# A layer norm moved to the head of VectorE's step, ahead of an earlier group's norm

## The reference

```
x = layernorm(x + sage(x, src, dst))        # three layers
x = layernorm(x + gat(x, edges))            # two attention layers
x = layernorm(x + jk(x, src, dst))          # four layers, maximum over them, one linear layer
x = layernorm(x + gcn(x, edges))            # three layers
```

## Time and profile before

| | |
|---|---|
| median of the runs | 7616.2 us |
| the profiled execution | 7673.8 us, span 7672.0 us |
| VectorE (DVE) | 4630.7 us busy, 60% of the span |
| TensorE (PE) | 4978.3 us busy, 65% |
| ScalarE (ACT) | 3048.8 us busy, 40% |
| GpSimd (POOL) | 3996.4 us busy, 52% |
| mean granted clock of TensorE | 0.798 |

### The profile page before, as it was taken

The page is one execution under the profiler, slowest core; times in us unless marked ns, Lnnn a source line. Parts: engine busy times, 40 slices in busy tenths (PEclk is TensorE's granted clock), DMA queues, the critical chain, the costliest instruction groups (busy, mean ns, idle before and its releaser), DMA issues. The chain is left out here.

```text
span 7672.0 us, 87356 instructions
## 1 busy us (share of the span) xinstructions
PE 4978.3 (65%) x23920; PEld 3346.6 (44%) x23924; DVE 4630.7 (60%) x13648; ACT 3048.8 (40%) x6979; POOL 3996.4 (52%) x3991
## 2 busy tenths in 40 slices
PE   6898887869989824676423444433799995579211
PEld 4666665535568602576322222221455553356111
DVE  4777666223356526667675456656899995545444
ACT  3555554533323202443343333333677773245000
POOL 4565554544344374655655655656233334654766
PEclk9999998989989755697555766766899998789555
DMA  6997665767756422686443466654577774566322
GB/s 146 236 243 231 204 207 175 238 194 243 234 179 202 124 53 53 173 249 190 127 119 105 128 112 119 120 105 87 206 246 257 246 258 152 170 184 176 88 87 72
DMA packets 1104143, 1292.18 MB, mean 168 GB/s; under 512 B 133903, under 2 KB 815679, under 8 KB 1097390
## 3 DMA queue, kind: packets, MB, share of 16 engines
q1 hardware_dynamic: 973518, 1032.63, 43.1%
q0 software_dynamic: 130144, 253.97, 15.5%
HBM read 607.93 MB, written 682.10 MB: 168 GB/s over the span
## 5 line engine op out<-in xcount | busy, mean ns | idle before, releaser
L573 POOL DMA_INDIRECT jk_layer_msg<-jk,idx_jk x588 | 590.0, 1003 | 374.9 <-issue 173.5
L1060 PE MATMUL jk_layer_sum_ps<-ident,jk_layer_weighted 128*128 128x128 f32 x784 | 172.1, 358 | 759.0 <-issue 392.2
L1060 PEld LDWEIGHTS jk_layer_sum_ps<-ident,jk_layer_weighted 128*128 128x128 f32 x784 | 110.2, 177 | 868.6 <-issue 447.6
L2089 POOL TENSOR_TENSOR rows_moved<-rows_x_in,w_lonely_row 128x512 f32<-128x512 f32 x98 | 124.5, 1271 | 685.8 <-DVE rows_x L674 639.8
L1082 DVE TENSOR_TENSOR_SCAN jk_layer_sum_t<-goes_on,jk_layer_sum_t,jk_layer_sum_ps 128x512 f32<-128x512 uint8 x196 | 250.1, 1276 | 346.5 <-DMA sage_nodes_x_in<-in_x 252.5
L1891 ACT ACTIVATE jk_layer_h_t<-jk_layer_h_ps,w_jk_b 128x512 f32<-128x512 f32 x196 | 134.7, 687 | 619.5 <-DMA gat_own<-yv 324.9
L699 PE MATMUL sage_nodes_h_ps<-sage_nodes_h_t,w_ws 128*128 128x512 f32 x784 | 363.2, 607 | 0.0
L573 POOL DMA_INDIRECT sage_end_msg<-h,idx x196 | 195.8, 999 | 290.5 <-ACT sage_end_weighted L1026 182.5
L1201 DVE COPY sage_h<-sage_turn 128x512 f32<-128x512 f32 x98 | 67.6, 690 | 452.7 <-PE sage_turn L690 343.2
L2288 PE MATMUL gcn_end_sum_ps<-ident,gcn_end_rows 128*128 128x128 f32 x196 | 54.6, 434 | 432.8 <-DVE gcn_end_rows L2281 214.5
L897 ACT ACTIVATE sage_nodes_h_t<-sage_nodes_h_ps,w_b_c 128x512 f32<-128x512 f32 x392 | 249.2, 690 | 207.5 <-PE sage_nodes_h_ps L699 105.0
(11 more groups left out here) (457 smaller groups left out, 16475.6 us busy)
## 6 DMA issues: line engine op xcount, KB each, us to landing
h<-sage_nodes_h SPq DMA_DIRECT2D x196, 512.0 KB
h_t<-sage_h_t SPq DMA_DIRECT2D x98, 512.0 KB
h<-sage_h SPq DMA_DIRECT2D x98, 512.0 KB
jk_t<-jk_layer_h_t SPq DMA_DIRECT2D x196, 256.0 KB
rows_layers<-jk_t SPq DMA_DIRECT2D x49, 1024.0 KB, 5.8
r<-rows_h SPq DMA_DIRECT2D x98, 512.0 KB
second_x_in<-u SPq DMA_DIRECT2D x147, 260.0 KB
jk<-jk_layer_h SPq DMA_DIRECT2D x147, 256.0 KB
```

The costliest lines, as they stand in the source:

```text
L573: pool.indirect_dma_start(out=into[:, g.number % depth, s, :], out_offset=None, in_=table, in_offset=bass.IndirectOffsetOnAxis(ap=index_ti ...
L1060: mm = pe.transpose(ps[:, c, at_s], self.weighted[:, g.b, s, c * P:(c + 1) * P], self.K.ident[:])
L2089: pool.tensor_tensor(moved[:, g.b], x_in[:, g.number % 3], to_subs(W.lonely_row), ALU.add).then_inc(lonely_added.sem, 1)
```

## The change

On VectorE, apply moves from the third place in the list to the first. Nothing else is touched: not its lag, its waits or its instructions, and no other engine.

```diff
@@ -2243,7 +2243,7 @@
             wait_for(dve, is_biased, g.lag(2))
             wait_for(dve, is_scaled, g.lag(2))
             s_norm.vector_apply(dve, g, s_y, s_z)
-        run_mixed(dve, [(apply0, 2, NODE), (add_slots, 4, SLOT), (apply, 10, NODE), (residual_sum, 8, NODE), (apply_slots, 7, SLOT),
+        run_mixed(dve, [(apply, 10, NODE), (apply0, 2, NODE), (add_slots, 4, SLOT), (residual_sum, 8, NODE), (apply_slots, 7, SLOT),
                         (top, 0, SLOT), (moments0, 0, NODE)])
     ph.close()
```

## The result

The changed kernel takes 7666.3 us (median of 4 runs, 7652.4 to 7672.8) against 7618.5 for the kernel before in the same comparison: ratio 1.006, 95% interval 1.0042 to 1.0078, slower by some 48 us.

What follows compares the result with a forecast made beforehand. VectorE was taken to set the pace, 19.95 us per pair; afterwards the wait for z's store would. 42 pairs at +0.75 us (+31.5) less 3 gave +28 us, 7616.2 to 7644 us, range 7606 to 7676.

Steps and rivals of the forecast that it cites:

- the sum: Phase rows3: 42 pairs of steps slower, +31.5 us, less 3 us for two pairs at TensorE's pace: +28 us.
- The stall removed: VectorE's apply: four tensor_scalars held by GpSimd's additions fall from 714 to 342 ns each; 146 us wasted now.
- What came back: VectorE beside GpSimd: residual_sum's addition loses 0.67 us in even steps; apply_slots' tensor_scalars take 1.80 us in odd steps.
- the loop: Even apply, end of top, load_layers and queue behind it, landing of z, next even apply; 20.7 us per pair.
- Even step to the end of top: VectorE's apply, apply0, add_slots, residual_sum and top in the even step: 8.93 us.
- Landing of z: Even groups' store of z, queued behind load_layers, lands 11.7 us after it; median 11.46, ends 11.2 and 13.4.
- The pair: An even and an odd step in rows3: 20.7 us, +0.75 against 19.95 now.
- TensorE's pace with the wait gone: Pair set by TensorE once its odd-step wait for ScalarE goes: 19.95 - 1.6 = 18.3 us.
- the pairs without layers: Two pairs after the 42, with no layers to load, go at TensorE's pace: -1.6 us each, -3 us.
- the faster rival: Store of z lands in time, only TensorE bounds: 18.3 us per pair, -73 us, 7543; chance 0.12.
- The rival that the two nearly cancel: No change: landing of 11.2 us, residual_sum not held 19.5 per pair, held 20.2; 7594 to 7624; chance 0.20.
- the one of the long landings: Slower still: z lands at 13.4 us, pair 22.4, +100 us, 7716; chance 0.08.

Runs made afterwards that it cites:

- the last experiment: Kernel before (apply in third place), GpSimd's additions add_bias and residuals made on one of four rows of a group only: 7595.6 us on another chip, ratio 0.9896.

## Why the prediction was right

The sign and the mechanism held, and the time of 7666.3 us lies within the range of 7606 to 7676, near its upper end. The loss was larger than the 28 us of the sum. Point by point:
- The stall removed: 714 to 343 ns per tensor_scalar, 342 expected. That GpSimd is its cause is shown by the last experiment.
- What came back: residual_sum's addition 1.35 us (1.36 expected), apply_slots 1.79 (1.80). What the odd step loses costs no time, since VectorE waits for z behind it anyway; what the even step loses is part of the loop.
- Even step to the end of top: 8.98 us, 8.93 expected.
- Landing of z: 11.7 us after load_layers is issued, 11.7 taken. It was right to go above the median of 11.46, as in a loop the late landings are not hidden; by how much was a judgement and no sum, and that it met is in part luck.
- The pair: 20.79 us, 20.7 expected. TensorE's pace with the wait gone: 18.2, where 18.3 was worked out.
- The sum is the term that was too small: 28 us expected, 35 in the profiled executions, 48 (32 to 60) in the runs. From the eighth load_layers to the last there are 41 gaps, one for each turn of the loop but its last (views by tile as above, before 5485 to 6330 us, after 5460 to 6330 us):

```profile
L2068 SPq DMA_DIRECT2D rows_layers<-jk_t x42: 319/320/320, 5490.4 to 6309.5; - x42
...
L2068 SPq DMA_DIRECT2D rows_layers<-jk_t x42: 319/320/320, 5465.5 to 6319.5; - x42
```

They took 6309.5 - 5490.4 = 819.1 us before and 6319.5 - 5465.5 = 854.0 after: +34.9 us, 0.85 per pair where 0.75 was taken. The rest of the phase took 996.3 - 819.1 = 177.2 us before and 1031.4 - 854.0 = 177.4 after, so of the 3 us that the pairs without layers were to give back nothing was left. There "behind step 98 other waits lead; I count nothing there" failed: with apply ahead, VectorE's wait for z near the phase's end rose from 9.3 us in three to 16.8 in five (6330 to 6440 us, before and after):

```profile
DVE rows_norm_root L671 <- DMA out<-rows_z: 9.3, 3, 4.1
...
DVE rows_norm_root L671 <- DMA out<-rows_z: 16.8, 5, 7.0
```

- One sign came out smaller: TensorE's wait in odd steps was to grow by as much as the pair. It grew from 58.8 / 40 = 1.47 us to 56.6 / 30 = 1.89 us. Much of what TensorE's pair is longer by lies in the matmuls themselves (5500 to 6200 us, before and after, columns as in the earlier trace rows):

```profile
5500.00:6200.00 700.00, 645.45 (x3032) 395.38 (x3031) 672.92 (x2491) 519.08 (x1056) 218.54 (x175) 1.00 0.72 250
...
5500.00:6200.00 700.00, 638.58 (x2890) 387.48 (x2891) 580.01 (x2397) 495.92 (x1010) 237.78 (x170) 0.97 0.69 240
```

By pairs of 19.99 and 20.79 us, TensorE is busy 18.4 us per pair before and 19.0 after, with the same matmuls, and the granted clock is 1.00 and 0.97. The last section shows one such fall of the clock.

The rule of the Trainium skill ("DMA: Bandwidth & Descriptors", section "Anatomy of one DMA — SWDGE (gpsimd) path"), by which 256 KB would take 2.6 us (an estimate), stood on the side of the faster rival. It is given there for one DMA that GpSimd issues; here SyncE issues z behind other transfers, the landings of 7.5 and 7.7 us decide, and the experiment with z two transfers ahead shows that z's time is its place in the queue.

The rival that the two nearly cancel failed at its condition: residual_sum is held, and the landing is 11.7 us, not 11.2. The faster rival needed a landing below 9.3 us, the one of the long landings 13.4.

## What to carry to other kernels

A wait that no view shows may have only little to spare: before a stage is moved ahead in an engine's order, ask of each of its waits when the thing it waits for really arrives, and subtract. For the store here that was set by what stands ahead of it in the issuing engine's list, with the wait in between, and not by its own size. Here the move was worth about 1% (ratio 0.991) once the store of z was issued ahead of the load that stands waiting, with no more memory; by itself it cost 0.6%.

## What the runs showed of the hardware beyond that

VectorE's two-input addition in SBUF gets in between two of GpSimd's additions. In the rows of the profile after it starts at 5981.10 and ends at 5982.45, not behind the last of GpSimd's additions but 0.54 us behind the one that runs, which ends at 5981.91. GpSimd's next is longer for it: 1.72 us at 5981.87, where the one before takes 1.27.

In the pair above TensorE's granted clock fell after its longer wait. The engine stood idle, then its first matmuls ran at a granted clock of 0.53 (busy by engine, then PEclk, in three stretches; then TensorE in order of time):

```profile
5978.00:5984.00 6.00, 6.00 (x36) 4.28 (x35) 5.83 (x25) 4.06 (x9) 4.18 (x3) 1.00 0.34 128
...
5984.00:5988.00 4.00, 1.31 (x4) 0.24 (x2) 3.90 (x16) 1.09 (x4) 0.00 (x0) 1.00 0.28 72
...
5988.00:5990.00 2.00, 1.98 (x3) 0.94 (x4) 1.93 (x8) 1.61 (x3) 0.52 (x1) 0.53 1.02 373
```

```profile
5984.29 1.02 PE L2125 MATMUL rows_h_ps<-rows_h_t,w_gcn 128*128 128x512 f32 x2
...
5988.02 2.00 PE L2127 MATMUL rows_h_ps<-rows_h_t,w_gcn 128*128 128x512 f32 x2 [2.71 <-ACT rows_h_t L2157]
```

0.53 of full speed is about the lower of its two levels (1.2 and 2.4 GHz). The engine had been idle from the end of its matmuls of 5984.29 until 5988.02, 2.71 us by the row, and the matmuls that take 1.12 us behind the shorter waits before took 2.00 us. The pair's time did not depend on it: VectorE waited for z until 5996.86. Behind the waits of 1.47 us before, the granted clock of 5500 to 6200 us was 1.00.
